# Moving the first tile table, batch 6's norm chain and the blank rows in an attention and mixture-of-experts kernel

## The reference, cut to what matters

```
x   : 8 batches x 512 tokens x 128 channels, float32
x   = x + attention(layernorm(x))                 # 16 heads of 8 channels, causal softmax
z   = layernorm(x)
top = top_2(z @ Wg)                               # 8 experts, softmax over the two scores, times alpha[e]
for e in range(8):
    h   = layernorm(z) * ln_w[e] + ln_b[e]
    y   = gelu(h @ fc1_w[e] + fc1_b[e]) @ fc2_w[e] + fc2_b[e]    # 128 -> 512 -> 128
    out = out + y * comb[:, e]
x   = x + out
```

## Time and profile before

| | |
|---|---|
| median of three runs | 543.2 us (542.79 to 543.74) |
| profiled execution | 541.11 us |
| its span | 539.3 us |
| PE busy | 470.3 us, 87% of the span |
| DVE, ACT, POOL busy | 366.5, 326.4, 366.6 us |
| attention ends, tiles begin | about 360 us |
| last matmul of the last tile | about 516 us |
| gather, last sums and stores | 519.7 to 539.3 us |

### The profile page before, as it was taken

The page is one execution under the profiler, slowest core; times in us unless marked ns, Lnnn a source line. Parts: engine busy times, 40 slices in busy tenths (PEclk is TensorE's granted clock), DMA queues, the critical chain, the costliest instruction groups (busy, mean ns, idle before and its releaser), DMA issues.

```text
span 539.3 us, 11883 instructions
## 1 busy us (share of the span) xinstructions
PE 470.3 (87%) x3296; PEld 273.3 (51%) x3296; DVE 366.5 (68%) x1284; ACT 326.4 (61%) x694; POOL 366.6 (68%) x712
## 2 busy tenths in 40 slices
PE   3469999999999999999999999787999899999820
PEld 1134444453444444444343444255888778888720
DVE  4588878899898899899889899752446432222226
ACT  2227787786686686786777676763545545555510
POOL 5956576587887887897897877856566556555420
PEclk9779999999999999999999999989999999999975
DMA  2323134134234233333223302247964688665349
GB/s 64 91 78 88 62 97 125 58 92 130 79 91 119 88 99 103 99 100 104 96 78 107 103 33 60 77 149 231 289 227 134 216 253 264 196 203 187 111 146 328
DMA packets 52728, 70.84 MB, mean 131 GB/s; under 512 B 11063, under 2 KB 38430, under 8 KB 52662
## 3 DMA queue, kind: packets, MB, share of 16 engines
q1 hardware_dynamic: 47478, 59.19, 36.3%
q0 software_dynamic: 4320, 8.53, 4.5%
q10 hardware_dynamic: 864, 2.36, 1.2%
HBM read 36.49 MB, written 20.94 MB: 106 GB/s over the span
## 4 chain that ended last, share of the span: by engine, by line
PE 52%; DVE 13%; POOL 12%; issue 10%; DMA 6%; ACT 3%; SPq 2%; another core or an unknown queue 1%; ACTq 0%; POOLq 0%; DVEq 0%
PE acc_bank L714 9%; PE acc_bank L782 8%; PE slots L682 8%; PE slots L773 8%; PE slots L699 7%; POOL probs L1303 4%; POOL z_dram L1286 3%; PE misc L650 3%; DVE masked L984 3%; DMA y_in<-y_dram 2%; PE slots L678 2%; PE misc L636 2%; DMA z_in<-z_dram 2%; PE slots L790 1%
## 5 line engine op out<-in xcount | busy, mean ns | idle before, releaser
L852 ACT ACTIVATE probs<-slots 128x512 f32<-128x512 f32 (+1 forms) x352 | 182.9, 562 | 69.0 <-PE slots L699 60.8
L984 DVE CUSTOM_DVE_ANT_0 masked<-slots,causal_row 128x512 bf16<-128x512 f32 (+1 forms) x256 | 147.1, 616 | 15.2 <-PE slots L682 15.1
L1303 POOL TENSOR_SCALAR_AFFINE_SELECT probs<-probs 128x128 f32<-128x128 f32 (+2 forms) x352 | 117.1, 351 | 39.3 <-ACT probs L852 34.5
L682 PE MATMUL slots<-stack_k,stack_q 125*128 125x256 bf16 (+3 forms) x512 | 128.3, 306 | 12.0 <-DMA stack_q<-parts 5.7
L699 PE MATMUL slots<-stack_q,stack_k 128*128 128x256 bf16 (+3 forms) x512 | 125.9, 302 | 1.8 <-DMA stack_q<-max_rows 1.8
L1334 POOL DMA_INDIRECT y_dram<-y,z_in x71 | 69.6, 981 | 55.0 <-DVE y L1163 17.2
L882 ACT ACTIVATE hidden<-slots,w_in 128x256 f32<-128x256 f32 (+1 forms) x156 | 62.0, 455 | 69.6 <-PE slots L773 59.8
L714 PE MATMUL acc_bank<-probs,v 128*32 128x512 f32 (+3 forms) x1024 | 95.5, 446 | 3.4 <-POOL probs L1303 3.3
L682 PEld LDWEIGHTS slots<-stack_k,stack_q 125*128 125x128 bf16 x512 | 47.9, 99 | 69.4 <-DVE row_max L984 29.7
L1286 POOL DMA_INDIRECT z_dram<-z,pos x64 | 63.5, 992 | 24.0 <-issue 14.0
L782 PE MATMUL acc_bank<-hidden,w_in 128*128 128x256 f32 (+1 forms) x312 | 69.6, 364 | 2.3 <-ACT hidden L882 1.4
(11 more groups left out here) (169 smaller groups left out, 522.8 us busy)
## 6 DMA issues: line engine op xcount, KB each, us to landing
w_in<-in_wpack SPq DMA_DIRECT2D x39, 516.0 KB
o_dram<-oT SPq DMA_DIRECT2D x32, 256.0 KB, 2.2
stack_k<-parts SPq DMA_DIRECT2D x95, 64.0 KB
stack_q<-parts SPq DMA_DIRECT2D x93, 64.0 KB
z_in<-z_dram SPq DMA_DIRECT2D x32, 132.0 KB
xt<-in_x SPq DMA_DIRECT2D x8, 256.0 KB, 3.0
onT<-o_dram SPq DMA_DIRECT2D x8, 256.0 KB
o_inv<-inv_dram SPq DMA_DIRECT2D x8, 256.0 KB
```

The source lines that it names most:

```text
L682: mm = pe.matmul(cols[:, i, :], q[0:K1, hh, blk * P:blk * P + P], k[0:K1, hh, 0:w], start=len(heads) == 1, stop=True, skip_group_check=True)
L852: act.activation(probs_of(n), columns(n, slot), ACT.Exp, scale=SCALE).then_inc(s_exp, 1)
L984: dve.tensor_tensor_reduce(out=masked[:, n % MASKED, 0:w], in0=slots[:, slot, 0:w], in1=causal_row[:, T - w:T], scale=1.0, scalar=NEG, op0 ...
L1303: pool.affine_select(out=diag, in_=diag, compare_op=ALU.is_ge, fill=0.0, base=0, pattern=[[0, len(heads)], [1, P]], channel_multiplier=-1) ...
```

## The change

All edits are in the tables and in the loops that fill the schedule; no instruction is added or taken away.

- **The first table and the first loads.** `t_count` to `t_row` move from places 359 to 363 to places 351 and 353 to 356; they now stand ahead of batch 6's `proj`, `r_stats` and `r_agg` on DVE. The loads of tiles 0 and 1 stood at place 366, those of 2 and 3 behind the attention loop; now all four stand at 363.
- **Batch 6's chain.** `r_root` goes from 361 to 376, behind the last unit's cut; `r_z` from 365 to 382; `zT`, `gate`, `r_copy`, `r_top`, `r_exp`, `r_comb` and `rank` go into the tile loop at places 0 to 5 (tiles 0 and 1). The projection goes one place back, the division by the sums two places ahead.
- **Dispatches of batch 6** start at tile 1 in place of two ahead of tile 0; the scatters behind them shift by up to two tiles and are back in step by tile 30.
- **Late table and blank rows.** `LATE_OTHER`: `t_count` and `pad_rows` go from place 31 (tile 10, place 1) to 26 (tile 8, place 2), the other steps by four or five places.
- **The residual of batch 7** moves from just ahead of the last `pv` to behind `fc2` of tile 0.

```diff
-LAST_BACK = {"residual": 40, "o_load": 45, "o_invert": 56, "o_spread": 61, "o_scale": 65,
-        "proj": 68}
+LAST_BACK = {"residual": 50, "o_load": 45, "o_invert": 56, "o_spread": 61, "o_scale": 65, "proj": 68}
...
-EARLIEST, FIRST_LOADS = 2, 366
-FIRST_TABLE, TABLE_STEP = 359, 1
+EARLIEST, FIRST_LOADS = 4, 363
+FIRST_TABLE = (351, 353, 354, 355, 356)
...
-BORDER_MOVES, LATE_DISPATCH_FROM = 2, 9
+EARLY_DISPATCH_FROM, LATE_DISPATCH_FROM = 1, 9
...
-    LATE_OTHER = {"t_count": 31, "t_span": 32, "t_owner": 34, "t_expert": 35, "t_row": 37, "pad_rows": 31}
+    LATE_OTHER = {"t_count": 26, "t_span": 28, "t_owner": 29, "t_expert": 31, "t_row": 32, "pad_rows": 26}
...
-        waiting = [("dispatch", EARLY_BATCHES, i) for i in range(BORDER_MOVES, 2 * NT)]
+        waiting = [("dispatch", EARLY_BATCHES, i) for i in range(2 * NT)]
...
-        for i in range(LARGE):
+        for i in range(EARLY_DISPATCH_FROM, LARGE):
...
-    add(("load", EARLIEST), *placed.pop(-1, []), *(("dispatch", EARLY_BATCHES, i) for i in range(BORDER_MOVES)), *(("load", i) for i in range(EARLIEST + 1, AHEAD)))
+    add(*placed.pop(-1, []))
```

More of the change, by code:

```diff
@@ L52 @@
 BY_SCALAR = (("stack", 0, 0, 1, 0), ("stack", 0, 0, 2, 0), ("stack", 0, 1, 2, 0))
-SOONER = {(6, "o_invert"): 8, (6, "o_spread"): 8, (6, "o_scale"): 8, (6, "proj"): 8, (6, "r_stats"): 8,
-          (6, "r_agg"): 10, (6, "r_root"): 8, (6, "r_z"): 8, (6, "zT"): 3, (6, "gate"): 3,
-          (6, "r_top"): 3, (6, "r_exp"): 3, (6, "r_copy"): 3, (6, "r_comb"): 6}
+SOONER = {(6, "residual"): 10, (6, "o_invert"): 8, (6, "o_spread"): 8, (6, "o_scale"): 10, (6, "proj"): 7, (6, "r_stats"): 6,
+          (6, "r_agg"): 8, (6, "r_root"): -7, (6, "r_z"): -9, (6, "zT"): -8, (6, "gate"): -6, (6, "r_copy"): -6,
+          (6, "r_top"): -2, (6, "r_exp"): -1}
 TABLE = ("t_count", "t_span", "t_owner", "t_expert", "t_row")
@@ L128, in build @@
             for i, step in enumerate(TABLE):
-                at(FIRST_TABLE + TABLE_STEP * i, step, 0)
+                at(FIRST_TABLE[i], step, 0)
         if b == B - 1:
```

4 lines of the change are left out of this document (2 added, 2 removed).

## The result

| | before | changed |
|---|---|---|
| median of five runs each | 543.2 us (542.79 to 544.25) | 549.89 us (547.29 to 552.05) |
| ratio, 95% interval | | 1.0131 (1.0098 to 1.0164) |
| span of the profiled execution | 539.3 us | 548.1 us |
| PE busy | 470.3 us | 476.0 us |

What follows compares the result with a forecast made beforehand. PE was taken to bound the tile phase (19.84 of 20 us busy). Border -3.5, blank rows +3.35 and half clock +1.7 summed to +1.5 us, so 543.2 became 544.7 us, range 539.5 to 548.

Steps and rivals of the forecast that it cites:

- Start of tile 0: End of attention: rows of tile 0 issued at 353.0, fc1 at 357.4 instead of 360.62, 3.2 us sooner.
- Tile 0 to tile 3: Tiles 0 to 3: fc1 of tile 3 sooner, 3.5 us gained, with a 1.65 us wait at yT of tile 1.
- The late gelu of tile 2: Ahead of fc1 of tile 3: if this lateness repeats, fc1 comes 3.0 us sooner instead of 3.85.
- The later steps of batch 6 stay off the path, all at nothing: Tile phase: batch 6's moved dispatches and scatters, batch 7's residual and the late table's operations cost nothing.
- The blank rows: Tile 13: a 5.3 us PE wait for its rows replaces 1.93 at tile 15; 3.35 us lost.
- its own bound: Blank rows at tile 13: 2.0 us lost if DVE reaches yT of tile 8 sooner by 1.4 us.
- Half clock behind a wait of 2 to 3 us: Behind PE's wait at tile 13: half clock adds 1.7 us lost, none to 3.4 as its ends.
- the clock stays full: Rival, behind the wait for tile 13: no half clock, 543.0 us; chance 0.12.
- the blank rows hold nothing: Rival, tiles 13 to 15: blank rows delay no load and the 1.93 us wait goes, 537.8 us; chance 0.16.
- the border did not give all it holds: Rival denied here, tiles 0 to 3: sums and gelu in time, 5.7 us gained, 542.5 us; chance 0.13.
- The moved chain becomes the wait: Rival, tiles 0 to 3: each queue late once more, gain 1.5 us or less, 546.8 us; chance 0.13.

Runs made afterwards that it cites:

- the border part: Run alone: the changed kernel with the late table and blank rows back at their old places; first run 530.88 us, ratio 1.0009 to the kernel before.
- job 2's trace: The changed kernel as it is, timed again beside the kernel before on another chip; 532.5 us, ratio 1.0013.
- the second pair of traces: The unaltered changed kernel and the kernel before, rerun in one job; changed 549.58 us, ratio 1.0100; before 542.09 us in one run.
- The sixteen halves: The changed kernel with each of the eight blank-row DMAs written as two of half the rows; 557.79 us in one run.
- job 3's trace of the kernel before: The kernel before, unaltered, run beside the changed kernel on a slower chip; 542.09 us in one run.
- two variants: The changed kernel with sixteen half blank-row DMAs, 557.79 us; and with batch 7's sums, scale and projection later and blank rows at their old place, 541.6 us.
- the pause on POOL: The changed kernel with a 0.2 us memset on POOL behind every indirect DMA of the tile phase; 531.64 us, ratio 1.0025; again 532.2 us, 1.0013.

## Why the prediction was right or wrong, point by point

**Start of tile 0: right.** Rows issued at 353.03 (predicted 353.0), transpose at 356.06 (356.3), fc1 at 357.46 (357.4). The landing of 3.3 us, taken from tile 15 because no weights stream ahead of it, was the right choice (3.0 measured). One thing was not in it: behind the wait of 1.85 us the clock was half, and fc1 of tile 0 took 3.36 us instead of 1.97. In none of the thirteen other traces with the border part, with waits of 0.98 to 1.87 us there, was it so.

**Tile 0 to tile 3: right in sum, by two errors, and so by luck.** fc1 of tile 3 came 3.55 us sooner (3.5 taken). The wait for yT of tile 1 was 0.76 us instead of 1.65, and the half clock made up for it. In the ten other traces that have the sums at the changed kernel's place that wait was 2.4 to 4.1 us, and by the medians of the border part alone the gain on those chips is nothing. In job 2's trace the sums were issued at 366.45 instead of 365.24, and PE, which had lost nothing to the clock, came 1.2 us sooner (369.04 instead of 370.22). In between stood what the step named, the wait for the sums (4.28 us of DVE) and batch 6's gate values, seven operations and 1.3 us ahead of yT. The late gelu of tile 2 was called possible chance. It was the first of the late signals, and the trace of before says so a few rows on, where `y` starts 1.9 us behind the end of its transpose:

```profile
373.25 0.38 PE L790 MATMUL slots<-ident,yT 128*128 128x128 f32 x2
```

```profile
375.56 0.42 DVE L1163 TENSOR_TENSOR y<-slots,z_in 128x256 f32<-128x256 f32 x1 [5.35 <-remote]
```

**"The later steps of batch 6 stay off the path, all at nothing": the step that failed.** The prediction put this term at 0. On the kind of chip that was measured, tiles 4 to 8 cost 7.6 us more (6.2 in the second pair of traces). What the step looked for, a result that comes too late for its reader, did not happen. What happened instead is that PE's fc1 was through by the profile, ACT and DVE were idle, and the first gelu started up to 5.9 us behind fc1 instead of 0.7; behind it PE waited 4.03 us and ran at half clock for 6.8 us. In the kernel before the same thing took place at moments when PE did not need the result: DVE's two "remote" waits for `y` add up to 10.3 us, of which 4.8 lie behind the ends of the transposes. The prediction read only the waits of PE and what PE waited for, and never asked why DVE still stood idle 1.9 and 2.9 us behind a finished transpose. A wait that costs nothing in one order can cost all its length in another, and a "remote" releaser on a one-core kernel was a sign that the profile could not explain a wait.

**The blank rows: right in kind, half in size.** The wait stands at tile 13, none at tile 15, half clock behind it. It was 2.93 us instead of 5.3, for three reasons. `ends` came 0.9 us sooner against PE's place: 0.76 us behind the start of fc1 of tile 9, where the prediction had 1.68. That was within its own bound; in the trace that it read, DVE had lost 1.61 us to a "remote" wait there. Then PE lost some 0.65 us behind the write of `ends`, at the transpose back of tile 10, with the late table's operations on DVE ahead of yT; on the other kind of chip tiles 8 to 12 likewise take 16.5 to 16.6 us with the sooner table and 15.9 without. And the distance from `ends` (408.70) to the transpose was 16.45 us instead of 17.04. (The whole stretch from tile 8 to 12 took 1.5 us longer, 17.4 instead of 15.9; the other 0.85 is half clock in fc1 of tile 8, left from the late signal.) Net the stretch from tile 12 to tile 15 cost 2.2 us, against 5.05 with its clock; the kernel before has 0.48 us of the table's delay in that stretch, so the blank rows alone cost some 2.6, 1.0 of waiting and 1.7 of clock. On the other kind of chip SP's block is 8.1 us instead of 9.4, the distance 14.4 to 15.0, the wait 0.9 to 1.4. The sixteen halves confirm the mechanism.

**Half clock behind a wait of 2 to 3 us: right here, but not a rule.** Behind 2.93 and 3.14 us the clock was half for 3.4 us, at the predicted price of 1.7. But at yT of tile 1, waits of 2.60, 2.70, 3.01, 3.14 and 4.14 us were followed by half clock and waits of 2.37, 2.90, 2.98 (twice) and 3.10 us were not. Nor is a shorter wait safe, as the prediction took it from the 1.93 us at tile 15: the same wait in job 3's trace of the kernel before was 2.09 us, with half clock behind it from 426.6 to 430.0. The Trainium skill (TensorE: Matmul & The Clock Gate, "HAM oscillation") tells of waits for DMAs that each put the clock back; these rows agree for some waits and not for others of the same length.

**The chances.** The sum from the steps it had would have been -3.6 + 2.2 = -1.4 us, or -0.8 with the 0.65 of the table: on the terms that it worked out, the prediction was too pessimistic by 2.3 to 2.9 us. That it forecast slower, and it became slower, is luck; it came out on the right side only through a term that it had at nothing (+7.6 up to tile 8, then +1.5 up to tile 12 and +1.1 behind tile 15; together with the two above +8.8 between the two profiled executions, of which that of before was 2.1 below its median). Of the rivals, "the clock stays full" and "the blank rows hold nothing" are refuted here, and the border did not give all it holds (3.6, where that rival needed over 5.05). "The moved chain becomes the wait" is what the 531 us kind shows at yT of tile 1, though not at the rows of tile 0, which were sooner there too. None of them had late signals in it.

**Still open.** What makes the signals late. That they fall into runs of POOL's indirect DMAs, on one kind of chip only, is seen in six traces of two kernels and two variants; that the runs cause it was not shown, since the runs' ends could as well be caused by it: POOL waits for PE's progress, too. The experiment meant to tell, the pause on POOL, never fell on such a chip. The Trainium skill (SBUF — State Buffer, "SBUF: two separate sides") has a rule by which DVE can hold up the descriptors of POOL's DMAs. The trace shows something else: ACT idle, DVE busy 0.98 of 4.91 us, POOL's issues at their usual 0.98 us each. No run here shows that rule at work. The loss between tiles 4 and 8 comes with the border part, but which of its pieces brings it (the moved dispatches, the moved chain or the sooner loads) is not known, since none was tried alone on that kind of chip; nor whether another program there would see the same.

## What to carry to other kernels

Before you cost a step at nothing, look at the idle time of the engines that are not the bound, and ask for each long wait whether its releaser had been done long before; such a wait is free only where it happens to stand. Do not compare a time from one chip with a trace from another: run both kernels in one job, and when a result is odd, run the pair again elsewhere before explaining it. And where a block of register-addressed DMAs goes on a queue that also feeds the bound engine, what counts is the time of the issues (here 1.0 to 1.3 us each with the register read, 0.6 without), so write what it waits for sooner and leave the block where the queue is ahead.

## What the runs showed of the hardware that was not expected

- Two kinds of chip: the same kernel takes 530.5 to 531.2 us (median, five jobs on four chips) or 543.2 to 543.6 (two measurements), with no difference up to the end of attention and all of it in the tile phase. Whether it is the chip itself or its state at the time is not shown.
- On the slower kind a first gelu starts up to 5.9 us behind fc1 instead of 0.7 to 0.8; in tiles 22, 24 and 26 it is 1.6 to 1.8 us in all six traces of that kind.
- The same block of eight blank-row DMAs on SP takes 8.0 to 8.2 us on the faster kind and 9.2 to 10.2 on the slower, where single register instructions of SP take up to 0.73 us and never over 0.19 on the other.
- Waits of PE of 2.4 to 3.1 us are sometimes followed by 3.4 us of half clock and sometimes not, in the same place of the same program.
